# A recommendation tower on one core: the Gram matrices of two samples in one matmul, and their useful blocks copied to SBUF

## What is computed

```python
e = jnp.stack([tbl_0[ids[:, 0]], ..., tbl_26[ids[:, 26]]], axis=1)   # (512, 27, 128)
dot_products = jnp.einsum('bnd,bmd->bnm', e, e)
z = dot_products[:, c, r]                                            # r, c = tril_indices(27, k=-1)
h = jnp.concatenate([z, dense_ctx], axis=1)
h = jnp.maximum(h @ W_top1 + b_top1, 0.0)
h = jnp.maximum(h @ W_top2 + b_top2, 0.0)
y = h @ W_top3
```

## Time and profile before

| what | us |
|---|---|
| median of 3 runs | 109.87 |
| lowest, highest of them | 109.17, 110.87 |
| profiled execution, span from the first to the last instruction | 123.6 |

### The profile page before, as it was taken

How to read it: one execution, slowest core, us unless ns; L and a number is a source line. 1 busy time by engine, 2 the same in 40 slices (tenths; PEclk the granted TensorE clock), 3 DMA queues, 4 the chain that set the end, 5 groups by cost and what they waited for, 6 DMA issues and landing times.

```text
span 123.6 us, 3473 instructions
## 1 busy us (share of the span) xinstructions
PE 106.3 (86%) x1496; PEld 86.1 (70%) x1496; DVE 70.0 (57%) x98; ACT 67.2 (54%) x112; POOL 68.1 (55%) x71
## 2 busy tenths in 40 slices
PE   6998799899999899999329993789458999997992
PEld 6534487687887687788219883669448999797891
DVE  6799999999999999999900050015001060103401
ACT  4596929899999999995200052025301144531442
POOL 3777888888888888887744166416560665000000
PEclk9999999999999999999985599558975699999999
DMA  3896366966984574711210101110200011000000
GB/s 79 262 237 190 101 204 146 293 198 155 302 235 111 172 229 108 205 48 42 54 52 17 31 29 42 27 48 21 66 24 27 21 48 41 23 5 5 5 0 1
DMA packets 5305, 12.06 MB, mean 98 GB/s; under 512 B 1765, under 2 KB 2277, under 8 KB 5290
## 3 DMA queue, kind: packets, MB, share of 16 engines
q1 hardware_dynamic: 3282, 7.75, 22.0%
q0 software_dynamic: 1984, 4.07, 12.8%
q10 hardware_dynamic: 24, 0.02, 0.1%
HBM read 11.83 MB, written 0.00 MB: 96 GB/s over the span
## 4 chain that ended last, share of the span: by engine, by line
PE 68%; DVE 16%; issue 13%; ACT 1%; DVEq 0%
PE ring L512 21%; PE gram_ps L539 12%; DVE marks L651 10%; PE gram_ps L512 8%; PE ring L592 5%; PE ids_ps L574 4%; PE ring L523 4%; DVE low L628 3%; PE ids_ps L567 2%; PE ids_ps L523 2%; PE ring L574 2%; PE ring L602 2%; PE ids_ps L592 1%; DVE pick L610 1%; PE ids_ps L553 1%
## 5 line engine op out<-in xcount | busy, mean ns | idle before, releaser
L422 POOL DMA_INDIRECT rows<-tbl,ids_sb x62 | 67.1, 1082 | 36.3 <-issue 15.9
L651 DVE TENSOR_TENSOR marks<-ids_ps,row_no 125x1024 fp32r<-125x1024 f32 (+2 forms) x39 | 43.5, 1148 | 0.0
L512 PE MATMUL ring<-marks,high 125*128 125x512 f32 (+1 forms) x64 | 26.6, 416 | 1.7 <-issue 1.6
L539 PE MATMUL gram_ps<-rowsT 128*27 128x27 f32 x1024 | 15.8, 206 | 11.4 <-issue 11.2
L512 PE MATMUL ring<-marks,low 125*128 125x512 f32 (+1 forms) x64 | 25.2, 394 | 0.0
L539 PEld LDWEIGHTS gram_ps<-rowsT 128*27 128x27 f32 x1024 | 13.3, 118 | 14.7 <-issue 14.0
L512 PEld LDWEIGHTS ring<-marks,high 125*128 125x128 f32 x64 | 12.8, 200 | 7.1 <-issue 4.6
L724 ACT ACTIVATE away<-ids_ps,row_no 125x512 f32<-125x512 f32 (+1 forms) x22 | 14.0, 715 | 4.7 <-PE ids_ps L466 4.1
L628 DVE TENSOR_TENSOR low<-raw,high 125x512 fp32r<-125x512 f32 (+1 forms) x23 | 16.2, 705 | 0.0
L672 DVE STREAM_TRANSPOSE gram<-gram_ps 128x416 f32<-128x416 f32 (+1 forms) x8 | 4.6, 612 | 18.1 <-PE gram_ps L539 18.1
L512 PEld LDWEIGHTS ring<-marks,low 125*128 125x128 f32 x64 | 12.9, 202 | 1.6
(11 more groups left out here) (61 smaller groups left out, 116.5 us busy)
## 6 DMA issues: line engine op xcount, KB each, us to landing
raw<-tbl SPq DMA_DIRECT2D x9, 448.0 KB
raw<-tbl SPq DMA_DIRECT2D x2, 560.0 KB
rows<-tbl,ids_sb POOLq DMA_INDIRECT x62
w_sb<-w SPq DMA_DIRECT2D x2, 256.0 KB
w_sb<-w SPq DMA_DIRECT2D x1, 512.0 KB
raw<-tbl SPq DMA_DIRECT2D x9, 52.0 KB
raw<-tbl SPq DMA_DIRECT2D x2, 224.0 KB
w_sb<-w SPq DMA_DIRECT2D x1, 192.0 KB
```

Of the source, the lines that this page charges most:

```text
L422: nc.gpsimd.indirect_dma_start(out=rows[0:n, i % ROW_BUFS, s, :], out_offset=None, in_=tables[PLACES[s]], in_offset=bass.IndirectOffsetOnA ...
L512: last = nc.tensor.matmul(bank[:, 0:n], part[:, i % SPLIT_BUFS, c * D:(c + 1) * D], mark_of(unit, c), start=c == 0 and part is high, stop= ...
L539: last = nc.tensor.matmul(gram_ps[s * STRIP:s * STRIP + F, g, 0:F], places, places, start=True, stop=True)
L651: nc.vector.tensor_tensor(marks_of(unit)[:, c0 - c1:, :], index.to_broadcast([TP, c1 - c0, n]), which.to_broadcast([TP, c1 - c0, n]), ALU. ...
```

## The change

Gram: the samples of a tile are numbered anew on the host, so that the four samples b to b+3 are those of the four strips. `rowsT` gets a pitch of 32, and a matmul takes two neighbouring samples: 64 stationary columns (2 x 32, the five spare ones cleared once by ACT) and 2 x 27 moving ones. Its result is 64x54, of which the two blocks of 27x27 on the diagonal are of use. Per tile there are 64 matmuls, 128 records, in place of 128 and 256. A part is 8 sample groups in one bank, as before four parts to a tile; the parts take the two banks in turn. After each part DVE copies the useful blocks of strips 0 and 1, and ACT those of strips 2 and 3, to `blocks` in SBUF, one 32x216 copy to a strip. PE waits with part n until both have copied part n-2. DVE's transposes wait for both and read `blocks`. The clearing of `gram_ps` is gone. `PACE` counts in quarters of a tile's Gram; the steps that it names are the same ones. `y_sb` lies over `fids`.

```diff
-F_PITCH = -(-F // PER_BANK) * PER_BANK
+WIDTH = [2, 2, 2, 2]
+GROUPS_IN = [1 << (BANK // (w * F)).bit_length() - 1 for w in WIDTH]
+GRAM_PARTS = [STRIP // g for g in GROUPS_IN]
+GRAM_BANKS = 2
...
-        rowsT = sb("rowsT", [P, B, F_PITCH])
+        rowsT = sb("rowsT", [P, B, STRIP])
...
+        def diagonal(i, part, strip, strips):
+            per, w = GROUPS_IN[i], WIDTH[i]
+            rows_of = slice(strip * STRIP, (strip + strips) * STRIP)
+            bank = gram_ps[rows_of, part_no(i, part) % GRAM_BANKS, 0:per * w * F]
+            at = strip % w * F
+            return (blocks[rows_of, part * per:(part + 1) * per, :],
+                    bank.rearrange("p (g m) -> p g m", g=per)[:, :, at:at + F])
...
-                    if of == "gram_part":
-                        pool.wait_ge(gram_part, value)
-                    if of == "products":
-                        pool.wait_ge(products, value)
+                    if of == "quarter":
+                        pool.wait_ge(gram_part, parts_through(value))
...
                         pe.wait_ge(taken, LAST_OF[i] + 1)
-                        if i >= 1:
-
-                            pe.wait_ge(regrouped, 2 * i)
-                    for g in range(part * STRIP // GRAM_PARTS, (part + 1) * STRIP // GRAM_PARTS):
-                        for s in range(n // STRIP):
-                            places = rowsT[:, b0 + s * STRIP + g, 0:F]
-                            last = nc.tensor.matmul(gram_ps[s * STRIP:s * STRIP + F, g, 0:F], places, places,
-                                                    start=True, stop=True)
-                    last.then_inc(products if part == GRAM_PARTS - 1 else gram_part, 1)
+                        if i == 0:
+                            pe.wait_ge(edges_ready, 1)
+                    if number >= GRAM_BANKS:
+
+                        pe.wait_ge(staged, number - GRAM_BANKS + 1)
+                        pe.wait_ge(staged_too, number - GRAM_BANKS + 1)
+                    for g in range(per):
+                        for s in range(0, P // STRIP, w):
+                            b = TILES[i][0] + (part * per + g) * (P // STRIP) + s
+                            last = nc.tensor.matmul(
+                                gram_ps[s * STRIP:(s + w) * STRIP, number % GRAM_BANKS, g * w * F:(g + 1) * w * F],
+                                rowsT[:, b:b + w, :].rearrange("p b f -> p (b f)"), rowsT[:, b:b + w, 0:F],
+                                start=True, stop=True)
+                    last.then_inc(gram_part, 1)
...
-            nc.vector.memset(gram_ps[:, :, :], 0.0).then_inc(gram_cleared, 1)
...
+                if kind == "gram":
+                    number = part_no(i, more[0])
+                    dve.wait_ge(gram_part, number + 1)
+                    for strip, strips in strips_of(i, 0):
+                        to, of = diagonal(i, more[0], strip, strips)
+                        last = nc.vector.tensor_copy(to, of)
+                    last.then_inc(staged, 1)
+                if kind == "gram" and is_last(*step[1:]):
                     n = TILES[i][1]
 
-                    dve.wait_ge(products, i + 1)
+                    dve.wait_ge(staged, number + 1)
+                    dve.wait_ge(staged_too, number + 1)
...
+            act.wait_ge(still_ready, 1)
+            nc.scalar.copy(rowsT[:, :, F:STRIP], still[:, 0:STRIP - F].rearrange("p (o f) -> p o f", o=1)
+                           .to_broadcast([P, B, STRIP - F])).then_inc(edges_ready, 1)
...
-                elif kind == "gram" and step[2] == GRAM_PARTS - 1:
+                elif kind == "gram":
                     n = TILES[i][1]
+                    number = part_no(i, step[2])
+                    act.wait_ge(gram_part, number + 1)
+                    if i >= 1 and step[2] == 0:
+
+                        act.wait_ge(regrouped, 2 * i)
+                    for strip, strips in strips_of(i, 1):
+                        to, of = diagonal(i, step[2], strip, strips)
+                        last = nc.scalar.copy(to, of)
+                    last.then_inc(staged_too, 1)
+                    if not is_last(i, step[2]):
+                        continue
```

More of the change, by code:

```diff
@@ L116, with part_no, parts_through, is_last @@
 PER_BANK = BANK // P
-F_PITCH = -(-F // PER_BANK) * PER_BANK
+WIDTH = [2, 2, 2, 2]
+GROUPS_IN = [1 << (BANK // (w * F)).bit_length() - 1 for w in WIDTH]
+GRAM_PARTS = [STRIP // g for g in GROUPS_IN]
+GRAM_BANKS = 2
+def part_no(i, part):
+    return sum(GRAM_PARTS[:i]) + part
+def parts_through(quarters):
+    i, q = divmod(quarters, 4)
+    return sum(GRAM_PARTS[:i]) + (q * GRAM_PARTS[i] // 4 if q else 0)
+def is_last(i, part):
+    return part == GRAM_PARTS[i] - 1
 GROUPS = [[range(g, min(g + PER_BANK, ng)) for g in range(0, ng, PER_BANK)] for ng in N_GATHERED]
@@ L156, in steps @@
     words = [w.split() for w in ORDER.replace("\n", ",").split(",") if w.strip()]
-    return [(kind, *(int(n) for n in at)) for kind, *at in words]
+    out = []
+    for kind, *at in words:
+        at = [int(n) for n in at]
+        if kind == "gram":
+            n = GRAM_PARTS[at[0]]
+            out += [(kind, at[0], part) for part in range(at[1] * n // 4, (at[1] + 1) * n // 4)]
+        else:
+            out.append((kind, *at))
+    return out
 STEPS = steps()
@@ L167 @@
 20 marks_used 15, 22 marks_used 18, 24 marks_used 20, 26 turned 4, 28 marks_used 25, 30 marks_used 27
-32 marks_used 30, 34 turned 6, 36 marks_used 35, 38 marks_used 38, 40 turned 9, 42 gram_part 2
-44 gram_part 3, 46 marks_used 50, 48 gram_part 5, 50 products 2, 52 l1_done 1, 54 gram_part 7, 56 paired 6
-58 products 3, 60 l1_done 7
+32 marks_used 30, 34 turned 6, 36 marks_used 35, 38 marks_used 38, 40 turned 9, 42 quarter 2
+44 quarter 3, 46 marks_used 50, 48 quarter 6, 50 quarter 8, 52 l1_done 1, 54 quarter 9, 56 paired 6
+58 quarter 12, 60 l1_done 7
 """
@@ L260, in build @@
         marks = sb("marks", [TP, MARK_BUFS, MARK_SIZE], F32R)
+        blocks = sb("blocks", [P, STRIP, F])
         gram = sb("gram", [P, F + K_STEPS, STRIP])
@@ L271, in build @@
         h2T = sb("h2T", [P, M2, P])
-        y_sb = sb("y_sb", [1, B])
+        y_sb = fids[0:1, :].bitcast(F32)
         ident = sb("ident", [P, P])
@@ L277, in build @@
         ids_ps = pb("ids_ps", [P, IDS_BANKS, BANK])
-        gram_ps = pb("gram_ps", [P, STRIP, STRIP])
+        gram_ps = pb("gram_ps", [P, GRAM_BANKS, BANK])
         ids_in = sem("ids_in")
@@ L293, in build @@
         row_no_ready = sem("row_no_ready")
-        gram_cleared = sem("gram_cleared")
+        edges_ready = sem("edges_ready")
         pick_ready = sem("pick_ready")
@@ L308, in build @@
         taken = sem("taken")
-        products = sem("products")
         gram_part = sem("gram_part")
+        staged = sem("staged")
+        staged_too = sem("staged_too")
         regrouped = sem("regrouped")
@@ L333, in ring_bank @@
                 return ids_ps[:, at - RING_BANKS - 2, :]
-            at = (at - RING_BANKS) * STRIP // 2
-            return gram_ps[:, at:at + STRIP // 2, :].rearrange("p g j -> p (g j)")
+            return gram_ps[:, at - RING_BANKS, :]
         def mark_of(unit, c):
@@ L352, in window, with strips_of @@
                            [list(start.ap[0]), [STRIP + 1, a1 - a0], [STRIP, K_STEPS]])
+        def diagonal(i, part, strip, strips):
[5 more added lines that the diff above has]
+                    bank.rearrange("p (g m) -> p g m", g=per)[:, :, at:at + F])
+        def strips_of(i, half):
+            return [(2 * half, 2)] if WIDTH[i] == 1 else [(2 * half, 1), (2 * half + 1, 1)]
         block = ctx.enter_context(nc.Block())
@@ L527, in _ @@
                 elif kind == "gram":
-                    b0, n = TILES[i]
                     part = step[2]
+                    w, per = WIDTH[i], GROUPS_IN[i]
+                    number = part_no(i, part)
                     if part == 0:
                         pe.wait_ge(taken, LAST_OF[i] + 1)
-                        if i >= 1:
-                            pe.wait_ge(regrouped, 2 * i)
-                    for g in range(part * STRIP // GRAM_PARTS, (part + 1) * STRIP // GRAM_PARTS):
-                        for s in range(n // STRIP):
-                            places = rowsT[:, b0 + s * STRIP + g, 0:F]
-                            last = nc.tensor.matmul(gram_ps[s * STRIP:s * STRIP + F, g, 0:F], places, places,
-                                                    start=True, stop=True)
-                    last.then_inc(products if part == GRAM_PARTS - 1 else gram_part, 1)
+                        if i == 0:
[11 more added lines that the diff above has]
+                    last.then_inc(gram_part, 1)
                 elif kind == "pairs":
@@ L662, in _ @@
                         mark(unit)
-                if kind == "gram" and more[0] == GRAM_PARTS - 1:
+                if kind == "gram":
+                    number = part_no(i, more[0])
[5 more added lines that the diff above has]
```

(6 more changed lines are left out.)

4 lines of the change are left out of this document (1 added, 3 removed).

## The result

The changed kernel takes **114.12 us** (median; 113.95 to 114.12 but for one) against 109.87: a ratio of **1.0395, interval 1.0345 to 1.0445**. It is slower by 4.2 us. Forecast were 111.3, +1.4. One execution of the five took 542 us, with PE busy for 538 us in place of 102, which nothing here explains, and it was the profiled one; no other run of this study did that, so the profile read here is of a second measurement of the same kernel (run `again`: 114.01, ratio 1.0436, interval 1.0387 to 1.0485). In the same way the profile of before that the prediction used, with its span of 123.6 us, turned out to be of an unusual execution, and a second one (run `before_again`) stands for it here.

The account below looks back on a forecast made before the run. POOL's gathers were taken to bound the kernel up to PE's last turn, PE after it. Tile 3's Gram +0.7, end +0.7, left over from tiles 0 to 2 +0.3, gap -0.3, start 0: +1.4, 111.3 us; range 107.3 to 114.3.

Parts of the forecast that it names:

- the slack: PE up to its last turn: ready at 87.9, POOL's data at 90.4, so some 2.5 us of delay absorbed.
- Rival C: PE becomes the bound, with wide Gram records at 31 ns: +5.1, 115.0 us; chance 0.14.
- Rival B: Gaps partly real, Gram issue-bound, tile 3's records staying at 9.6 ns: -2.4, 107.5 us; chance 0.25.
- The gaps in the profile are not in the runs: PE's 11.2 us of issue gaps before the Gram are the cost of recording; runs are mostly free of them.
- POOL's floor: POOL's gathers without waits, plus PE's work from the last turn on: 106.1 us, 3.8 under the runs.
- A wide record takes 24.5 ns: Gram matmuls: near the streaming bound of 23.8, upper end 31; 3.15 us a tile, 0.7 more than before.
- Half the records save nothing in steady state: Gram: twice the array area is computed and half thrown away, so a tile costs 0.7 us more.
- The transposes read SBUF, which I cost at nothing: DVE's two transposes after a tile's Gram: 1.15 us for both, unchanged when reading SBUF.
- The copies: DVE and ACT after each Gram part: pairs of 0.55 and 0.65 us; only tile 3's last part exposed, +0.7.
- The end: After tile 3's Gram: DVE's transposes, windows and h2T come 0.7 us later, nearly all reaching the end.
- Tile 0 to tile 1: PE's wait for ACT's copy of find 11, ahead of tile 1's Gram, grows to some 0.9 us.
- Start: Dropped bank clearing and ACT's new 3 us clearing of spare columns: counted 0, upper end 1 to 2 us.

Follow-up runs that it names:

- half_moving: The changed kernel with 27 instead of 54 moving columns, the second sample's own products left out: 113.84 us in one run.
- turned: The changed kernel with `blocks` laid out [27, 32], sample group innermost, so DVE's transposes read SBUF without a step: 110.96 us, ratio 1.0158.
- one_wide_turned: The changed kernel with one sample to a matmul in all tiles and `blocks` laid out [27, 32]: 109.20 us, ratio 0.9983 against before.
- one_wide: The changed kernel with one sample to a matmul in all tiles; copies to SBUF, pitch of 32 and ACT's clearing kept: 111.81 us, ratio 1.0238.

## Why the prediction was wrong

The direction was right and the size was not: +4.2 us came where +1.4 stood, and "within 2%" had the largest chance. The step that failed is the slack. The sum let 2.5 us of PE's delay up to the last turn be absorbed and left 0.3; there was no slack, and 2.8 us came through. With no slack, the prediction's own terms give +4.1. Beside it two costs were wrong: the transposes' read of SBUF, put at nothing, cost 3.05 us, and a wide record, put at 24.5 ns, took 31.3. They show so little in the total because issue gaps of 2.4 us went with the change, which the sum counted at 0.3.

The measured time lies inside the range, near its upper end. Rival C (115.0: PE bound, 31 ns a record) had both of its conditions right. That its time is only 0.9 us off is partly luck: it too absorbs 2.5 us that weren't there, and it has no term for the transposes or for the gaps. Rival B was right that part of the gaps is real and goes, and wrong on the records, which did not stay at 9.6 ns.

1. *The gaps in the profile are not in the runs*: right for all but 2.4 us of them. Its reason, "the cost of recording", was wrong: the second profile records the same 1,024 records, and its span fits its time. The 13.7 us belonged to one disturbed execution. Of the 3.8 us left over above POOL's floor, 1.9 lie around the span, and they are no gaps.

2. *PE has 2.5 us of slack up to the last turn*: wrong. I had PE at its last turn at 87.9 without its gaps, and POOL's data ready at 90.4. In the second profile the turn starts at 90.73, and PE has not waited for POOL. The last gather:

```profile
87.80 0.95 POOL L422 DMA_INDIRECT rows<-tbl,ids_sb  x1 [0.30 <-issue]
```

With the 2.9 us from gather to turn of the earlier trace rows, POOL's data are there at 90.7 by estimate. So POOL's side was right to 0.3 us, and PE came 2.8 us later than I had it. I had subtracted all gaps, but 1.8 us of them up to this place are real, and had taken the best stretch, 9.6 ns, for all tiles, where narrow records come up to 15 ns apart in tiles 0 to 2 (192 in 2.9 us from 67.04 on). That PE would come 3.0 us later to its last turn after the change was forecast, and 2.8 were measured, but this is luck: the waits for ACT grew by 2.6 us where 0.9 stood, the Gram by 1.9 where 2.1 stood, and the gaps fell by 1.8 where nothing stood.

3. *A wide record takes 24.5 ns*: 31.3, my upper bound of 31. The step from streaming (23.8 ns) was the wrong bound to be near: halving the moving columns changes the record by 0.4 ns (half_moving). Still, the width costs only 1.8 us in all (turned 110.96 against one_wide_turned 109.20). In the profiles of these two runs PE's Gram stretches sum to 16.3 and 12.6 us, the issue gaps to 0 and 1.9, and its other waits from 56 us on to 1.6 in both. So the 1.8 us are the records less the gaps, and the smaller parts and more numerous copies that come with the width add nothing to PE's waits. *Half the records save nothing in steady state* was right. The Trainium skill's rule (TensorEngine Tiling (Array Packing), section Instruction Overhead), by which 54 moving columns cost what 27 do, agrees for records with 64 stationary columns (30.9 and 31.3 ns) and less well for those with 32 (9.6 and 13.0). The Gram did not get cheaper by it, because a record with the wider stationary side costs more than the halved count gives back.

4. *The transposes read SBUF, which I cost at nothing*: wrong, +0.8 us a tile and 3.05 us in all (turned). This is the largest single cost. In the runs, DVE's transpose with a step of 27 floats in SBUF takes 1,017 ns against 602 without, and its copies from PSUM take 373 ns in runs of 27 or with a step of 54. The Trainium skill has a rule for the first (SBUF — State Buffer, section Specifications (TRN2)): SBUF has lines of 16 bytes, full bandwidth needs at least two hits in a line, and each crossing to a new line pays. With a step of 27 floats every element is in a new line, and the trace agrees, though no run here separates the lines from the step. The earlier trace rows had shown a ratio of 2:1 for ACT's writes, and I used it for the clearing and not for the transposes.

5. *The copies*: pairs of 0.76 and 0.67 us where 0.55 and 0.65 stood, exposed once a tile; with one sample to a matmul they cost nothing measurable (one_wide_turned). *The end*: +0.7 forecast; PE's wait is 1.25 us there and 0.5 in turned. Right in kind, short by the transposes. *Tile 0 to tile 1*: 0.9 us forecast, 1.6 measured, 0.8 in turned. Again right but for the transposes.

6. *Start*: right, 0, with 2.84 us for the clearing against 3.

The parts, from differences of runs: strided transposes 3.05 us (again less turned), width 1.8 (turned less one_wide_turned), copies, clearing and pitch nothing measurable (one_wide_turned against before). Taken in the other order, the width is 2.2 (again less one_wide) and the transposes 2.6 (one_wide less one_wide_turned). Either way they make up the 4.75 us between `again` and before, within 0.1.

## What to carry to other kernels

When an edit moves an operand from PSUM to SBUF, look at the step of its innermost run first: here one changed layout of the buffer in between was worth 3 us of 114, more than the matmuls that the edit was about. Slack is not to be computed by subtracting gaps from a disturbed profile: here that gave 2.5 us where there was none, so take a second profile of the kernel before you subtract. And work that stands between a result and its next reader on PE may be cover: moving it away put a wait of 2.2 us where one of 1.6 had been.

## What the runs showed that I had not expected

- A float32 matmul record with 64 stationary columns in two halves of the array took 31 ns with 27 or with 54 moving columns; with 32 stationary columns in four strips 9.6 ns with 27 and 13.0 with 54. All four are from the first half of the last tile, at a granted clock of 1.0; elsewhere narrow records came up to 15 ns apart.
- DVE's 32x32 transpose of 448 columns: 602 ns from SBUF without a step, 1,017 ns with a step of 27 floats; from PSUM with a step of 32 two transposes took the same 1.15 us as without a step from SBUF.
